# The attention spread of a recommendation kernel: one 128-column matmul for both partition halves

## What is computed

```python
cand = candidate @ Wi + bi                       # [512, 64]
hist = history @ Wi + bi                         # [512, 200, 64]
hidden = relu((cand @ Wq)[:, None, :] + hist @ Wk)
scores = where(mask, hidden @ Wv, -1e9)          # [512, 200]
attn = softmax(scores, axis=1)
interest = einsum('bs,bse->be', attn, hist)      # [512, 64]
avg = sum(hist * mask) / length
x = concat([interest, cand, avg])                # then three layers with batch norm, relu, sigmoid
```

## Time and profile before

| | |
|---|---|
| time, median of 3 runs | 221.59 us (221.26 to 221.71) |
| time of the profiled execution | 222.31 us |
| its span, first to last instruction | 220.2 us |
| PE busy | 206.5 us (94%) |
| PEld busy | 81.1 us (37%) |
| DVE busy | 174.7 us (79%) |
| ACT busy | 103.7 us (47%) |
| POOL busy | 62.5 us (28%) |
| spread matmuls (L430) | 512 records, 472 of them to attn_ps, 40 to hist_ps |

### The profile page before, as it was taken

One profiled execution on the slowest core, in us unless ns is written; L12 is line 12 of the kernel. 1 busy time (PEld: TensorE's weight loads), 2 busy tenths in 40 slices (PEclk: granted clock), 3 DMA queues, 4 the chain that ended last, 5 costly groups with the idle time before them and its releaser, 6 DMA issues.

```text
span 220.2 us, 6280 instructions
## 1 busy us (share of the span) xinstructions
PE 206.5 (94%) x2110; PEld 81.1 (37%) x2110; DVE 174.7 (79%) x1087; ACT 103.7 (47%) x302; POOL 62.5 (28%) x112
## 2 busy tenths in 40 slices
PE   6899999999999999999999999999999998976593
PEld 2432333334343433333434343343434433423321
DVE  0327665897979797979797998979797979798970
ACT  2025545355546363645555453555463635552423
POOL 8903014060606050413224150606060503322000
PEclk9999999999999999999999999999999999999955
DMA  5999999696969797887969696969697870000000
GB/s 172 374 422 419 419 308 323 253 315 225 336 216 328 255 307 277 277 319 265 320 222 326 231 324 255 315 227 338 208 343 244 290 293 4 0 3 0 4 0 0
DMA packets 10225, 53.72 MB, mean 244 GB/s; under 512 B 1105, under 2 KB 2001, under 8 KB 10194
## 3 DMA queue, kind: packets, MB, share of 16 engines
q1 hardware_dynamic: 10194, 53.32, 69.3%
HBM read 53.32 MB, written 0.00 MB: 242 GB/s over the span
## 4 chain that ended last, share of the span: by engine, by line
PE 87%; DVE 5%; DMA 2%; issue 2%; ACT 2%; SPq 1%; DVEq 0%; ACTq 0%
PE hist_ps L388 43%; PE key_ps L401 24%; PE score_ps L412 10%; PE attn_ps L430 5%; DVE scratch L533 3%; DMA history<-history_dram 2%; DVE kept L520 1%; PE score_ps L462 1%; PE score_ps L457 1%; PE score_ps L454 1%; ACT x L320 1%; ACT hidden L300 0%; PE attn_ps L370 0%; PE key_ps L443 0%; PE hist_ps L430 0%
## 5 line engine op out<-in xcount | busy, mean ns | idle before, releaser
L300 ACT ACTIVATE hidden<-key_ps,query 128x200 f32<-128x200 f32 x256 | 88.6, 429 | 92.9 <-PE key_ps L401 92.9
L388 PE MATMUL hist_ps<-history,params 128*64 128x400 f32 x512 | 103.0, 523 | 2.5 <-DMA history<-history_dram 1.6
L520 DVE SCALAR_TENSOR_TENSOR kept<-item,lens,hist_ps 128x200 f32<-128x200 f32 x256 | 93.8, 418 | 13.9 <-PE hist_ps L388 13.9
L533 DVE CUSTOM_DVE_ANT_0 scratch<-attn_ps,kept 128x200 f32<-128x200 f32 x236 | 72.1, 362 | 17.6 <-PE attn_ps L430 17.6
L401 PE MATMUL key_ps<-kept,params 64*64 64x400 f32 x512 | 58.2, 523 | 2.2 <-ACT hidden L300 1.4
L388 PEld LDWEIGHTS hist_ps<-history,params 128*64 128x64 f32 x512 | 30.9, 138 | 43.7 <-issue 26.4
L254 POOL TENSOR_SCALAR attn<-weights,inv_sum 128x200 f32<-128x200 f32 x15 | 6.5, 435 | 122.2 <-DVE inv_sum L548 122.2
L401 PEld LDWEIGHTS key_ps<-kept,params 64*64 64x64 f32 x512 | 13.8, 132 | 42.6 <-issue 34.5
L412 PE MATMUL score_ps<-hidden,wv_rows 128*32 128x200 f32 x512 | 25.1, 336 | 0.0
L430 PE MATMUL attn_ps<-parts,spread 64*64 64x200 bf16 x472 | 21.2, 250 | 2.6 <-DVE parts L620 2.2
L430 PEld LDWEIGHTS attn_ps<-parts,spread 64*64 64x64 bf16 x472 | 13.3, 106 | 24.4 <-issue 15.9
(11 more groups left out here) (67 smaller groups left out, 57.8 us busy)
## 6 DMA issues: line engine op xcount, KB each, us to landing
history<-history_dram SPq DMA_DIRECT2D x63, 800.0 KB, 5.0
history<-history_dram SPq DMA_DIRECT2D x2, 400.0 KB, 4.9
candT<-candidates_dram SPq DMA_DIRECT2D x1, 256.0 KB, 5.4
params<-parameters_dram SPq DMA_DIRECT2D x1, 248.5 KB, 12.2
params<-parameters_dram SPq DMA_DIRECT2D x1, 226.5 KB, 2.5
lens_raw<-lengths_dram SPq DMA_DIRECT2D x1, 136.0 KB, 4.1
probability<-result SPq DMA_DIRECT2D x1, 2.0 KB
```

The costliest lines, as they stand in the source:

```text
L300: act.activation(hidden[:, g % HID_SLOTS, v, :], key_ps[:, v, at * SEQ:(at + 1) * SEQ], ACT.Relu, bias=query[:, 2 * g + v:2 * g + v + 1]). ...
L388: product = pe.matmul(hist_ps[64 * h:64 * h + 64, g % 2, 0:QCOLS], param("wi"), history[:, slot, h, 2 * at:2 * at + 2, :].rearrange("f p s ...
L520: dve.scalar_tensor_tensor(out=kept[:, g % KEPT_SLOTS, u, :], in0=item[:, :], scalar=pair_len[:, col:col + 1], in1=hist_ps[:, g % 2, u * S ...
L533: dve.tensor_tensor_reduce(scratch[:, at, v, :], banks[:, at, v * SEQ:(v + 1) * SEQ], kept[:, q % KEPT_SLOTS, v, :], 1.0, 0.0, ALU.mult, A ...
```

## The change

The loop over h is gone. One matmul takes the weight columns of both h (two neighbouring rows of 64 entries of `spread`, seen as 128 columns) and writes all 128 partitions of the bank. A spread is then four matmuls in tiles of 64 rows by 128 columns (two such tiles cover the array) in place of eight in 64 by 64 tiles. What is written to PSUM is the same, and no semaphore, wait or place in an engine's stream changes.

```diff
                 for v in range(2):
                     for at in range(2):
                         rows = slice(64 * at, 64 * at + 64)
-                        for h in range(2):
-                            product = pe.matmul(banks[64 * h:64 * h + 64, at, v * SEQ:(v + 1) * SEQ],
-                                                spread[rows, TILE_ROWS * v + 2 * k + h, :], parts[rows, j % 2, :],
-                                                start=True, stop=True)
+                        row = TILE_ROWS * v + 2 * k
+                        product = pe.matmul(banks[:, at, v * SEQ:(v + 1) * SEQ],
+                                            spread[rows, row:row + 2, :].rearrange("p h e -> p (h e)"),
+                                            parts[rows, j % 2, :], start=True, stop=True)
                 product.then_inc(attn_spread, 1)
```

## The result

| | before | changed |
|---|---|---|
| median | 221.65 us (4 runs, 221.26 to 222.05) | 223.62 us (4 runs, 223.28 to 224.0) |
| ratio to before | | 1.0097, 95% interval 1.0072 to 1.0121 |
| profiled execution, its span | 222.31 us, 220.2 us | 224.0 us, 221.9 us |

The change costs 1.97 us (by the interval 1.6 to 2.7 us). 224.2 was forecast, in a range of 222.6 to 227.2. A ratio leaves out the runs that are over 1.5% above the fastest of their kernel, in experiment 12 seven of twelve, so it is not always the ratio of the medians.

A forecast was written before the change was run, and what follows sets the result against it. PE was taken to bound the kernel. Border +4.4, load and rounds -0.4, DVE holes -1.1, unit 60 -0.2, tail -0.1 sum to +2.6 us: 224.2 us against the 221.59 median, range 222.6 to 227.2.

The forecast's parts named there:

- The new border: Keys (64*64) to spread (64*128) becomes a change of tile shape on PE: 40 x 0.11 = +4.4 us.
- The load: In spreads, 128-column bfloat16 weights load fast, showing 0.014 us across a border; with the rounds, -0.4 us in all.
- slow-load rival: Fast load doesn't come with row tiles, so 0.053 us show per spread: +4.6 us, 226.2 us; chance 0.22.
- Two rounds: A wide spread keeps two rounds of 0.083 us, as two 64*128 tiles cover the array and matmuls overlap in pairs.
- What DVE gives back: PE's waits for DVE shrink: 13 holes after spreads go, -1.1 us, and the wait at unit 60 shortens, -0.2 us.
- Sum of the long stretch: From the second score's start to the last keys' start: the terms 4.4 - 0.4 - 1.1 - 0.2, without the tail.
- The tail: After 197 us: +0.1 us ahead of DVE's chain, -0.2 to -0.3 where spread and L443 share a shape; together -0.1 us.
- The free border: Rival: keys to spread costs no border when only columns change; 221.1 us, chance 0.07.
- A round more: Rival: spread pairs don't run together, 0.167 us more on 54 spreads, +9, 233 us; chance 0.09, shared with full-length loads.

The follow-up runs named there:

- experiment 12: The changed kernel unaltered, measured again beside the others on one chip; ratio 1.0044 to the kernel before, median of all 12 runs 224.44 us.
- experiments 1 and 2: Changed kernel with one half of each spread wide (64*128), the other narrow (64*64): wide first 232.06 us, narrow first 226.88 us.
- experiment 5: Changed kernel with all four matmuls of a spread reading the first row half alone; 234.73 us, ratio 1.0594 to the kernel before.
- experiment 3: Changed kernel with 127 of the 128 weight columns in all spreads but the first; 227.33 us, ratio 1.029 to the kernel before.
- Experiments 6 and 7: The kernel before and the changed one, each with DVE's multiply-and-sum (L533) over 100 of the 200 items; 216.58 and 220.84 us.
- experiment 4: Changed kernel with the spread's loops over v and at exchanged, so two matmuls of one row half follow each other; 224.04 us, ratio 1.0149.
- experiment 9: The kernel before with the exchange: spread ahead of score in units that have both; median 219.38 us beside 221.57 for the kernel before.
- experiment 8: The kernel before with wide spreads only after a score and from the last superblock's score on; median 220.51 us beside 221.57.

## Why the prediction was right

- *The new border*, +4.4 us from 40 x 0.11. Measured 0.835 - 0.722 = 0.113 us, 40 x 0.113 = 4.5 us. The row that carried it was the one step from 64*64 to 64*128 at 203.80; experiments 1 and 2 show that the cost goes with the change of shape, once for each, and moves with it. The loads of the wide spread begin only when the spread does, where the narrow ones stood 0.33 us ahead. Whether the 0.11 us are a drain of the array or something else between two shapes, no run here tells apart; the Trainium skill ("TensorEngine Tiling (Array Packing)", "Key Properties") calls it a drain and gives no figure.
- *The load*, 0.014 us by the warm-up row, against 0.053 for the slow-load rival. Loads of 94 ns were measured (95 forecast), the spread after keys lasts 0.275 us (0.28), after a score 0.275 (0.276). Together 40 x 0.007 + 14 x 0.02 = 0.6 us where 0.4 was forecast. What the rival describes is what experiment 3 shows with 127 columns: 132 ns (133 forecast), 0.316 us.
- *Two rounds*: confirmed by experiment 5, which has four. The reason that I gave, pairs that overlap, holds.
- *What DVE gives back*: forecast 1.1 us of holes and 0.2 us at unit 60. The 40 spreads after keys give 13.16 - 11.57 = 1.59 us, of which 40 x 0.007 = 0.3 are the shorter spread; the remaining 1.3 us are 1.1 of holes and 0.2 of the wait (0.71 to 0.49). Experiments 6 and 7 show the same sum from the other side, 1.15 us.
- *Sum of the long stretch*: 4.4 - 0.4 - 1.1 - 0.2 = 2.7 forecast, 2.66 measured (4.5 - 0.6 - 1.1 - 0.2). The 41st border costs its 0.11 us too, and the wait for ACT behind it gives that back (1.78 to 1.66), as the count of 40 supposed. That the sum is this close is in part luck: the border came out 0.1 higher and the spreads 0.2 lower than forecast. A superblock takes 11.92 us (from the score at 36.59 to the one at 48.51; 11.9 forecast).
- *The tail*, -0.1 us: measured -0.2. The spread at 211.66 went from 0.48 us to 0.31 (213.69 to 214.00), and L443 behind it from 1.00 to 0.87 us (214.00 to 214.87), that is 0.3 us, at the upper end of the forecast. The 0.1 us ahead of it is there: from the last keys to L457 it is 11.58 us before and 11.66 after.
- *The free border* (0.07) would have needed keys to spread at 0.72, and it is at 0.835. *A round more* would have needed 0.45 us.

The measured +1.97 lies 0.6 under the forecast +2.6, and experiment 12 has +2.9 by its medians. The mechanisms come to 2.66 - 0.2 = 2.4 or 2.5 us in the traces; the rest is of the size of what the start and the end of single executions move by, and the first interval (1.6 to 2.7) holds both.

## What to carry to other kernels

Count the changes of tile shape in PE's stream before counting matmuls: here each that was measured costs 0.11 to 0.13 us at full clock, more than a whole round of 200 bfloat16 columns (0.083 us), and halving the matmuls of a group gained 0.007 to 0.02 us. Put groups with the same tiles next to each other; moving one call past another gave 2.2 us where the wider matmul lost 2.0. And where a second engine is close behind the first, look for its holes before adding a cost up: 1.3 of 4.5 us came back from there.

## What the runs showed that was not expected

**Matmuls of different row halves seem to pass each other.** In experiment 4 the program gives two matmuls of the lower row half and then two of the upper. By experiment 5 two of one half take their rounds one after the other, and yet four took two rounds (0.278 us, +0.003). Two rounds for four matmuls need one of each half in a round, so one of the upper half must have run beside the first of the lower, ahead of the second. This is concluded from the two runs and not seen: the records don't name the half.

**127 columns are slower to load than 128**, 132 against 94 ns.

**A gain in the middle can be eaten at the end by the clock.** The kernel before with the exchange is 2.7 us faster in the long stretch (experiment 9) and only 2.2 in the time. Granted clock (the third value from the right) in stretches behind the last keys, first of the kernel before (last keys at 198.45), then with the exchange (194.59):

```profile
207.00:209.00 2.00, 1.32 (x18) 0.48 (x18) 1.81 (x13) 0.00 (x0) 0.00 (x0) 1.00 0.03 8
209.00:211.00 2.00, 1.55 (x11) 0.33 (x10) 2.00 (x17) 0.72 (x1) 0.00 (x0) 0.76 0.00 0
```
```profile
203.00:205.00 2.00, 1.19 (x17) 0.58 (x18) 1.81 (x11) 0.00 (x0) 0.00 (x0) 0.86 0.03 8
205.00:207.00 2.00, 1.67 (x11) 0.23 (x10) 1.93 (x15) 0.72 (x1) 0.00 (x0) 0.50 0.00 0
```

In both, PE has idled in part of the time after the last keys, and the clock then goes from 2.4 to 1.2 GHz. In the first it does so 11.6 us behind the last keys, in the second 9.9 us behind them, and what follows the last keys lasts 21.7 and 22.5 us. One matmul holds the whole difference:

```profile
208.25 0.97 PE L454 MATMUL score_ps<-x,params 128*64 128x448 f32 x2
```
```profile
204.39 1.76 PE L454 MATMUL score_ps<-x,params 128*64 128x448 f32 x2
```

Both start 9.80 us behind the last keys. The second runs into the lower clock, 0.79 us longer, and L457 behind it stands 12.37 us behind the last keys where it stood 11.58.

The start moves too. The first long group of projections after the queries, in the kernel before and in the hybrid (experiment 8):

```profile
12.05 2.88 PE L388 MATMUL hist_ps<-history,params 128*64 128x400 f32 x8
```
```profile
11.83 2.01 PE L388 MATMUL hist_ps<-history,params 128*64 128x400 f32 x8
```

Both run the same instructions up to there; in the second PE came to its upper rate earlier in the group (at the upper rate the next eight records take 1.56 us). In the changed kernel's first trace the same group takes 2.55 us, and by the next projection it is 0.67 us ahead of the kernel before (15.30 and 15.97 us), nearly the whole of the 0.71. Between the traces the second score starts anywhere from 35.9 to 38.2 us. The two traces of the changed kernel have the same long stretch to 0.02 us; up to it they take 36.59 and 38.19 us, behind it 21.5 and 20.6. So the scatter comes from the start and the end, as far as traces show, and a change of 1% is better weighed in the middle. What makes the clock rise or fall sooner in one execution than in another was not tried.

**The row of the clock can be wrong at the start.** The first projection in the kernel before, then in the changed one:

```profile
5.71 1.60 PE L388 MATMUL hist_ps<-history,params 128*64 128x400 f32 x4 [1.12 <-DMA history<-history_dram]
```
```profile
5.55 0.89 PE L388 MATMUL hist_ps<-history,params 128*64 128x400 f32 x4 [1.22 <-DMA history<-history_dram]
```

The same four records take 1.60 us where the PEclk row of the kernel before has a 9 in its second slice, and 0.89 us where that of the changed kernel has a 6. 0.89 us is also what four of them take inside the superblocks, at full clock (120.94). So the 679 in the changed kernel's row doesn't mean that its start was slower: by the lengths of its groups it was the faster one. Ahead of the first change that a row shows, go by the matmuls.
